# Attention in rounds of four score blocks: the third round at the seam of two heads, joint denominators, maxima transposed ahead of the last blocks, roots spread over places

## What is computed

```
x = x + scan(norm(x)); x = x + experts8(norm(x))
x = x + attention(norm(x)); x = x + experts32(norm(x))

# attention, for each batch and head
q, k, v = x Q, x K, x V            # 1024 x 64
att = where(causal, q k^T * scale, -inf)
y = softmax(att) v
z += y W
```

## Time and profile before

| what | value |
|---|---|
| median of 3 runs | 2235.08 us |
| profiled execution, its time | 2246.38 us |
| its span, first to last instruction | 2244.5 us |
| mean granted TensorE clock | 0.929 |
| TensorE busy | 1962.5 us (87%) |
| VectorE, GpSimd, ScalarE busy | 1361.9, 1174.6, 1074.7 us |
| attention stage | from about 605 to 1957 us |

### The profile page before, as it was taken

The page is one execution under the profiler, slowest core; times in us unless marked ns, Lnnn a source line. Parts: engine busy times, 40 slices in busy tenths (PEclk is TensorE's granted clock), DMA queues, the critical chain, the costliest instruction groups (busy, mean ns, idle before and its releaser), DMA issues. The chain is left out here.

```text
span 2244.5 us, 42930 instructions
## 1 busy us (share of the span) xinstructions
PE 1962.5 (87%) x11815; PEld 1459.2 (65%) x11816; DVE 1361.9 (61%) x3630; ACT 1074.7 (48%) x2250; POOL 1174.6 (52%) x1159
## 2 busy tenths in 40 slices
PE   4852999999699999999999999999999999965760
PEld 2542888888466676677777677777677777643660
DVE  6766344434467776656786646786657777553652
ACT  5322333333455555555655555655555655411760
POOL 3454223332225556536677736677735677732673
PEclk8765999999799999999999999999999999977885
DMA  9652333333411112112221112211112211122978
GB/s 335 212 196 79 50 52 49 51 50 52 118 47 52 49 53 55 41 27 58 63 60 49 37 29 58 56 47 49 37 27 58 56 48 47 28 94 92 210 136 256
DMA packets 206555, 177.56 MB, mean 79 GB/s; under 512 B 85506, under 2 KB 188503, under 8 KB 205728
## 3 DMA queue, kind: packets, MB, share of 16 engines
q1 hardware_dynamic: 175984, 142.97, 21.3%
q0 software_dynamic: 28656, 27.61, 8.1%
q10 hardware_dynamic: 1728, 4.73, 0.5%
HBM read 95.05 MB, written 80.72 MB: 78 GB/s over the span
## 5 line engine op out<-in xcount | busy, mean ns | idle before, releaser
L932 POOL TENSOR_TENSOR c_den<-c_den,c_p 128x512 f32<-128x512 f32 (+3 forms) x576 | 550.4, 956 | 349.0 <-ACT c_p L1235 278.1
L1235 ACT ACTIVATE c_p<-PS 128x512 f32<-128x512 f32 (+3 forms) x768 | 350.2, 487 | 326.4 <-PE PS L2438 219.3
L2459 PE MATMUL PS<-c_p,c_vh 128*64 128x256 f32 (+1 forms) x2816 | 335.6, 352 | 0.0
L2407 PE MATMUL PS<-c_k,c_q 128*128 128x512 f32 (+2 forms) x768 | 287.0, 374 | 12.5 <-DVE c_max L1802 5.4
L2430 PE MATMUL PS<-c_q,c_k 128*128 128x512 f32 (+2 forms) x768 | 292.9, 385 | 2.8 <-issue 1.6
L2459 PEld LDWEIGHTS PS<-c_p,c_vh 128*64 128x64 f32 x2816 | 198.1, 137 | 105.5 <-issue 51.8
L2431 PE MATMUL PS<-c_q,c_k 128*128 128x512 f32 (+2 forms) x768 | 258.8, 348 | 0.0
L874 POOL DMA_INDIRECT acc<-b_y,b_tok x71 | 110.5, 1557 | 277.1 <-ACT b_y L1113 254.9
L1226 ACT ACTIVATE c_q<-PS 64x512 fp32r<-64x512 f32 x256 | 151.2, 591 | 167.5 <-PE PS L2394 164.2
L1802 DVE CUSTOM_DVE_ANT_0 PS<-PS,c_maskq 128x128 f32<-128x128 f32 (+3 forms) x256 | 126.9, 500 | 152.6 <-PE PS L2407 145.3
L1802 DVE CUSTOM_DVE_ANT_0 PS<-PS,c_maskq,c_max 128x128 f32<-128x128 f32 (+3 forms) x256 | 143.1, 559 | 105.0 <-PE PS L2407 79.4
(11 more groups left out here) (293 smaller groups left out, 3945.4 us busy)
## 6 DMA issues: line engine op xcount, KB each, us to landing
c_vh<-c_v SPq DMA_DIRECT2D x64, 256.0 KB
c_rrow<-rden SPq DMA_DIRECT2D x63, 256.0 KB, 3.6
routed<-b_empty SPq DMA_DIRECT2D x32, 289.0 KB, 9.1
d_xe<-routed SPq DMA_DIRECT2D x32, 289.0 KB
b_xt<-routed SPq DMA_DIRECT2D x71, 130.0 KB
b_w12T<-in_w12T_dram SPq DMA_DIRECT2D x16, 512.0 KB, 11.8
acc<-X SPq DMA_DIRECT2D x16, 512.0 KB
X<-acc SPq DMA_DIRECT2D x16, 512.0 KB, 6.8
```

What stands on the lines that cost most here:

```text
L932: pool.tensor_tensor(c_den[c][:, off:], c_den[c][:, off:], p, ALU.add).then_inc(s_cPa, 1)
L1235: act.activation(c_p[:, P_AT[m]:P_AT[m] + WIDTH[m]], PS[:, ST_BANK[m % ROUND], skip:skip + WIDTH[m]], ACT.Exp, scale=ATT_SCALE).then_inc(s ...
L2407: pe.matmul(PS[:, 2 + use[0], 0:max(w, 256)], c_q1[h][:, t * P:(t + 1) * P], c_k1[h][:, c * 512:c * 512 + max(w, 256)], start=True, stop=T ...
L2459: ins = pe.matmul(dst, c_vh[h][:, j, :], moving, start=(j == 0), stop=(t0 == 2 + a))
```

## The change

A round has four blocks (ROUND = 4), so a head has three: blocks 0 to 3 (the early half), 4 to 7, and 8 to 11. The third round stands at the end of the head's list, behind the next head's first three blocks; nothing is multiplied between the projections and those. The three banks of the transposed scores keep their rotation (STB = 3). c_p grows from 2688 to 3328 columns, with one layout for each parity of the head (R_AT). Denominators of both halves are computed together, in the next head behind M7, in bank 7; c_den of the early half has one buffer for each parity, of the late half one. `transpose_max` stands directly behind the second round, ahead of blocks 9 to 11, and ScalarE's `take_max` ahead of the exponential of block 9. On VectorE the inversion stands behind M7, and the second low split of keys behind M11. The roots of batch 0 are cut into thirteen steps (`late_root`), one at each place from head 5 to head 8. xn[0] shares its memory with the routing's r_xT, and waits for the DMA that stores that.

```diff
-        ROUND = 3
+        ROUND = 4
...
+        R_SIZE = [sum(WIDTH[r * ROUND:(r + 1) * ROUND]) for r in range(ROUNDS)]
+        P_SIZE = R_SIZE[0] + R_SIZE[1]
+        R_AT = ((0, R_SIZE[0], 0), (R_SIZE[1], 0, R_SIZE[1]))
+        ST_BANK = (4, 5, 1)
+        STB = len(ST_BANK)
...
+                    if c > 0 and j == 0:
+                        if nxt or hd + 1 < NH:
+                            copy_k(H + 1, 1 - h)
+                        continue
...
                     elif j == 1 and c > 0:
+
+                        pool.wait_ge(s_cD, H + 2)
...
+            def make_xn(batch, g):
+                if g == 0 and not (isinstance(batch, int) and batch <= 1):
+                    act.wait_ge(s_dxs, batch * 32 - 32)
...
+            def late_root(n):
+                st.sync()
+                if n == 0:
+                    st.done(dve.tensor_scalar(late_var, late_var, 1.0, EPS, ALU.mult, ALU.add))
...
+                elif n < RSQRT_STEPS + 1 and n % 3 == 0:
+                    st.done(dve.tensor_tensor(late_tmp, late_rstd, late_rstd, ALU.mult))
+                elif n < RSQRT_STEPS + 1 and n % 3 == 1:
+                    st.done(dve.scalar_tensor_tensor(late_tmp, late_tmp, -0.5, late_var, ALU.mult, ALU.mult))
+                elif n < RSQRT_STEPS + 1:
+                    st.done(dve.scalar_tensor_tensor(late_rstd, late_tmp, 1.5, late_rstd, ALU.add, ALU.mult))
...
+                    n = (hd - 5) * 4 + (place - 1) if splits(b) else -1
+                    if 0 <= n <= RSQRT_STEPS + 1:
+                        late_root(n)
...
-                if splits(b) and hd + 3 == NG:
-                    ready_rstds(QT, NT - QT)
...
-            def denominators(H, c):
-
-                pe.wait_ge(s_cPa, H * len(BLOCKS) + (2 * ROUND + (4, len(BLOCKS))[c]))
-                if c == 0:
-
-                    pe.wait_ge(s_cyn, H * (2 * NC2) + 3 * NC2)
-                for g in range(4):
-                    ins = pe.matmul(PS[g * 32:(g + 1) * 32, 6, 256:384], c_pick[:, c, :], c_den[c][:, g * P:(g + 1) * P],
-                                    start=(c == 0), stop=(c == NC2 - 1))
+            def denominators(H, h):
+
+                pe.wait_ge(s_cPa, H * len(BLOCKS) + (2 * ROUND + len(BLOCKS)))
+                pe.wait_ge(s_cyn, H * (2 * NC2) + 4 * NC2)
+                for c in range(NC2):
+                    for g in range(4):
+                        ins = pe.matmul(PS[g * 32:(g + 1) * 32, 7, 256:384], c_pick[:, c, :], c_den[c][h][:, g * P:(g + 1) * P],
+                                        start=(c == 0), stop=(c == NC2 - 1))
```

More of the change, by code:

```diff
@@ L254, in network @@
         c_p = place("c_p", [P, P_SIZE])
-        c_den = [place(f"c_den_{c}", [P, 512]) for c in range(NC2)]
+        c_den = [[place(f"c_den_{h}", [P, 512]) for h in range(2)], [place("c_den_late", [P, 512])] * 2]
         c_max = place("c_max", [P, QT])
@@ L259, in network @@
         c_yT = [place(f"c_yT_{n}", [P, S]) for n in range(2)]
-        xn = [place(f"xn{g}", [P, G, D]) for g in range(S // GT)]
+        xn = [None, place("xn1", [P, G, D])]
         c_spread = nc.alloc_sbuf_tensor_at("c_spread", [P, 4, NC2, DQ], F32, offset=at[0] - 4 * G * D)
@@ L931, in head_adds @@
                         pool.sem_inc(s_pass, 1)
[L932 to L935, removed]
+                        pool.tensor_tensor(den[:, off:], den[:, off:], p, ALU.add).then_inc(s_cPa, 1)
+                    if route and m % 3 == 2:
                         for n, a in enumerate(ROUTE_AT):
-                            k = (hd - a - 6) * 4 + m // ROUND
+                            k = (hd - a - 6) * 4 + m // 3
                             if 0 <= k < G * K1:
@@ L1350, in _ @@
             take_first_v(14, 15)
-            for m in range(ROUND):
-                probabilities(0, m)
+            for m in range(STB):
+                probabilities(0, 0, m)
             batch_exps(0, False, True)
@@ L1975, in head_steps @@
                     maxima(9)
-                    for k in range(2 * more):
-                        split_lo(H + 2, h, 0, k)
-                        maxima(10 + k)
-                    if not more:
-                        maxima(10, 11)
+                    if more:
+                        split_lo(H + 2, h, 0, 0)
+                    maxima(10, 11)
+                    if more:
+                        split_lo(H + 2, h, 0, 1)
                 routing(2)
@@ L1984, in head_steps @@
                     normalise_y(pair - 1, c_yT[1 - hp % 2])
-                else:
-                    routing(3)
+                routing(3)
                 maxima_ahead(2, 3)
@@ L2422, in scores_t @@
                 n = WIDTH[m] + skip
-                bank = ST_BANK[m % ROUND]
+                bank = ST_BANK[m % STB]
                 diagonal = j * P >= c * 512
@@ L2548, in outputs_of @@
                             pe.wait_ge(s_cyn, H * (2 * NC2) + (2 * c + 2))
-                            if c == 0 and hd:
+                            if c and hd:
                                 pe.wait_ge(s_cr, H)
@@ L2557, in head_products @@
                 maxima(5)
-                if hd:
-                    denominators(H - 1, 1)
                 scores_t(H, h, 5)
@@ L2563, in head_products @@
                     transpose_x(b + 1, 0, table)
-                    maxima(7, 8)
+                    maxima(7)
+                    denominators(H - 1, 1 - h)
+                    maxima(8)
                 else:
@@ L2567, in head_products @@
                     maxima(7)
+                    if hd:
+                        denominators(H - 1, 1 - h)
                     projections(1)
@@ L2585, in head_products @@
                 outputs_of(1)
+                if follows:
+                    transpose_max(H + 1, table)
                 for m in (9, 10, 11):
@@ L2589, in head_products @@
                 mask_t(9, 10, 11)
-                if follows:
-                    transpose_max(H + 1, table)
                 if fetch:
@@ L2600, in head_products @@
                 maxima_ahead(1)
-                denominators(H, 0)
-                outputs_of(2)
                 maxima_ahead(2)
```

72 lines of the change are left out of this document (40 added, 32 removed).

## The result

The changed kernel takes **2218.45 us** (median of 4 runs, 2215.3 to 2219.39) against 2234.75 us in the same comparison: ratio 0.9915, 95% interval 0.99 to 0.9929. It is faster, by 16 to 22 us. I had forecast 2242.0 and a range from 2225 to 2256, and given "faster" a chance of 0.23: the sign was wrong and the range missed it.

A forecast was written before the change was run, and what follows sets the result against it. TensorE's instruction list was taken to bound the attention stage. Savings of -33.9 us and waits of +40.8 summed to +6.9 us on the profiled 2246.4, giving 2242.0 us on the median, range 2225 to 2256.

The forecast's parts named there:

- (e): Transposed maxima, now behind a 4-byte group instead of the mask: 0 to 0.1 us a head, +3 us, from 0 to 8.
- (a): Six heads with VectorE's slot arithmetic ahead of chunk 0's maximum: 0.9 us of new wait each, +5.4 us.
- (b): ScalarE's routing rows delay block 10's exponential; the next head's block 1 waits 0.7 us in three heads: +2.1 us.
- (c): Batch ends: the last head's joint denominators wait for ScalarE's copies of y, 1.2 us four times, +4.8 us.
- merging the rounds: In each head five 4-byte groups become four, with joint denominators: 0.42 us a head saved, -27.1 us (-22 to -29).
- roots: Batch 0, head 5: spreading the root operations removes TensorE's stall and the low clock behind it, -6.8 us (-3 to -7).
- wait at N2 and N3: Chunks 2 and 3 of the maxima ahead wait for VectorE, 0.33 us in 62 heads: +20.5 us (+11 to +25).
- (d): Chunk 6 in twelve heads of batch 0, no longer covered by denominators, waits 0.4 us more each: +5 us.
- Rivals 1 and 5: First: chunk 2 does not wait, 2221.5 us, chance 0.11. Second: the merge saves nothing, +27 us, chance 0.06.
- rival 4: Batch ends and waits in every head lower TensorE's clock: +7 us, 2249; chance 0.17 together with port collisions.
- Rival 3: Spread roots and normalisation collide with GpSimd's adds at shared ports: +7 us, 2249; chance 0.17 together with the clock.
- rival 2: (a), (b), (d), (e) and half of (c) overlap: 2224 us at the least, 2233 with half; chance 0.24.

## Why the prediction was wrong, point by point

The forecast was a sum of +6.9 us; the stage came out at -18.6. The large terms were right. What failed is the sum of the small ones: (e) with the wrong sign, (a), (b) and (c) as waits that did not come or came smaller, and a gain at M4 that was in no term. The terms, with what the traces and runs give in their place:

| term | forecast | measured |
|---|---|---|
| merging the rounds | -27.1 | about -30: the groups as priced, joint denominators 0.57 for 0.62 |
| roots | -6.8 | -6.3 in the head, +1.3 at M6 of two others; undone, 3.9 and 1.3 |
| wait at N2 and N3 | +20.5 | about 21, and 3 more at block 0 in batches 1 and 2 |
| (a) slot arithmetic | +5.4 | under 1 |
| (b) routing rows | +2.1 | 0 |
| (c) batch ends | +4.8 | 2.7 of waits in three ends; moving them gave 1.75 |
| (d) M6 in batch 0 | +5 | about 4, and the 1.3 of the roots |
| (e) transposed maxima | +3 | -5.6, of which undoing shows half |
| wait at M4 | not in the sum | -3.6 |

What is left, some 6 us of gain, is in small pieces that I can't separate from the spread between runs: z products that take 1.54 us behind the denominators where they took 1.64 (in every second head, some 3 us in all), projections of batch 0, and 1.2 us in its first head. The last is luck: it is a low-clock stretch that this trace lacks and most of the others have, and at batch 0's fetching head 1.0 us was lost by the same cause.

**The large steps held.** The 4-byte groups have the predicted lengths. The main new wait stands where it was put, with its two parts: N1 takes 0.34 us on the mean instead of 0.12, N2 0.10 more than its columns. The low weights ahead of M6 cost what the rows said, and moving them gave all of it back. Moving them took the roots' 1.3 us away too. Rivals 1 and 5 are refuted. The waits at N2 brought no low clock (rival 4): from the first chunk to the last the clock is granted 0.50 in three stretches of 3.4 us, at the three fetching heads, where before it was three of 3.4 us (the first head and the last two fetching heads) and the one of 6.8 behind the roots.

**The step that failed most is (e).** I priced the transposed maxima by what stands around them and took "0 to 0.1 a head" as a loss. Their piece got 0.56 us longer where the round alone is 0.65 longer, so 0.09 a head were gained; half of this, 0.046 in the median head, is the transposition's own place, as undoing it showed. What gives the other half stays open. I had also never computed the chain that starts there: 2.8 us from the transposition to block 0. That error had no effect on the sum, since the change moved both. It would have had one in any variant, 31 us.

**(a) was priced by a row that was itself disturbed.** VectorE reached N0 late in the earlier trace rows, by 1.6 us, behind four small operations. These rows are of the kernel before, first VectorE's last three of the four, then GpSimd's adds:

```profile
1098.60 1.02 DVE L1907 TENSOR_SCALAR r_skip<-r_pos 128x16 f32<-128x16 f32 x1
1099.65 0.18 DVE L1909 TENSOR_TENSOR r_skip<-r_skip,r_pos 128x16 f32<-128x16 f32 x1
1099.86 0.94 DVE L1911 SCALAR_TENSOR_TENSOR r_slot<-r_idx,r_skip 128x16 uint32<-128x16 f32 x1
```

```profile
1098.29 1.29 POOL L932 TENSOR_TENSOR c_den<-c_den,c_p 128x512 f32<-128x512 f32 x1 [0.47 <-POOL c_den L932]
1099.77 1.01 POOL L932 TENSOR_TENSOR c_den<-c_den,c_p 128x384 f32<-128x384 f32 x1 [0.18 <-POOL c_den L932]
```

The same operations of the changed kernel:

```profile
1084.73 0.36 DVE L1941 TENSOR_SCALAR r_skip<-r_pos 128x16 f32<-128x16 f32 x1
1085.12 0.18 DVE L1943 TENSOR_TENSOR r_skip<-r_skip,r_pos 128x16 f32<-128x16 f32 x1
1085.33 0.18 DVE L1945 SCALAR_TENSOR_TENSOR r_slot<-r_idx,r_skip 128x16 uint32<-128x16 f32 x1
```

```profile
1083.77 1.29 POOL L942 TENSOR_TENSOR c_den_late<-c_den_late,c_p 128x512 f32<-128x512 f32 x1 [0.18 <-POOL c_den_late L942]
```

Each of these small operations that starts while an add of GpSimd runs ends 0.02 to 0.04 us behind that add: 1099.62 behind 1099.58, 1100.80 behind 1100.78, 1085.09 behind 1085.06. Started between two adds, it takes 0.18. Not every operation of VectorE is held: a reduction of 128 x 512 elements from 1084.01 on ran its 0.69 us while the add of 1083.77 was under way. In the new order the adds lie differently, and VectorE reaches N0 on time in these heads (0.46 us behind TensorE, 0.82 at worst, against 1.52 to 2.13). The Trainium skill (SBUF - State Buffer, "SBUF: two separate sides") states such a lock for a VectorE operation with two SBUF inputs, or in a mode that uses two ports, against one of GpSimd. The trace agrees, and here an operation on a single tensor is held too (the 1.02 us); whether it ran in such a mode, no row tells. I had quoted that rule against the roots and not seen that it had inflated the price of (a). How much of (a) came from that, and how much from the later N0, no run separates. The low weights of (d) show the same: of their 16 subtractions in the changed kernel seven began during an add and took 1.27 us, the other nine took 0.42.

**Rival 3 was half right.** The roots' steps took 0.17 to 1.08 us, by the same collision. One of them in its place ahead of M4's maximum, VectorE, GpSimd, TensorE:

```profile
758.23 0.74 DVE L1773 TENSOR_TENSOR rstds_tmp<-rstds 128x24 f32<-128x24 f32 x1
```

```profile
758.19 0.74 POOL L942 TENSOR_TENSOR c_den<-c_den,c_p 128x256 f32<-128x256 f32 x1 [0.17 <-POOL c_den L942]
```

```profile
759.75 0.50 PE L2440 MATMUL PS<-c_k,c_q 128*128 128x512 f32 x1 [0.93 <-DVE c_max L1829]
```

At M6 of two heads TensorE waited 0.67 us longer for that: 1.3 us, not 7, because the other places have slack.

**The wait at M4 was overlooked.** In the kernel before, M4 stood 0.13 to 0.28 us in 29 heads (5.4 us in sum), waiting for VectorE to be done with what was last in its bank. With N2 directly behind N1 and a longer round behind N3, VectorE is ahead in all but 10 heads (1.8 us). Delaying the chunks N2 and N3 by a block made it 42 heads and 7.1 us, so their place decides it; what the longer round adds was not tried alone.

**Waits overlap (rival 2), and more than I allowed.** (b) vanished while N2 waited, and appeared, with up to 0.7 us in each of six heads, when N2's wait was taken out and block 1 came earlier. Rival 2 gave 2224 "at the least", and the result lies below, since its floor still held (e) at zero.

## What to carry to other kernels

A sum of one well-measured large term and several small waits, each priced as if TensorE came on time, leans to one side: the first wait pays for the next. Before an edit is called a cost or nothing, compute the chain that starts at it to its consumer in the new order. A change that removes work between two such points can live from a small edit beside it, as this one did (31 us). A wait can also cost more than its own time: five waits of 2 us were each followed by 3.4 us at a granted clock of 0.50. And a duration taken from one row should be held against the same instruction elsewhere, when another engine shares its memory.

## What the runs showed of the hardware

- A VectorE operation on 128 x 16 or 128 x 24 elements took 0.17 us, or up to 1.09 us when it started beside an add of GpSimd; it then ended within 0.04 us of the add.
- A product that waited for a semaphore cost 0.10 us beyond the wait at M6 of batch 0 (M6 to M7 0.80 us instead of 0.70). At M4 it did not: in 29 heads of the kernel before, M4 waited 0.13 to 0.28 us, and M4 to M5 took 0.80 us instead of 0.78.
- Eight denominator records in front of a round took 0.35 us; sixteen in one group took 0.57, so eight more added 0.22, not 0.27.
- With idle times of 1.9 to 2.0 us ahead of one product, in six heads of the kernel with the routing rows behind block 2, the granted clock fell to 0.50 for 3.4 us in five of them.
- On a chip where the program outside the stage took 879 us instead of 922, the stage was the same within 1.5 us.
